# Slot order in a fused image and text transformer block: row maxima, projections, sum of values, drain

## The chip, the cores and the metric

The kernel runs on one core of a Trainium2 chip. The metric is the device time of one execution in microseconds (us). The core has five engines that work side by side and wait for each other by semaphores: TensorE (PE, matrix products and transposes; PEld is its weight load), VectorE (DVE), ScalarE (ACT), GpSimd (POOL) and SyncE (SP), which here only issues transfers.

## The reference

16 images with 16 text rows each go through four stages. All is float32.

```
h = edges(gray(x)) + text rows                      # per image 256 rows of pixels and 128 of text, 256 wide
h = h + attention(layernorm(h))                     # 16 heads of 16, window of 128 keys, 1e-9 added to each weight
n = layernorm(h); h = h + (n, and gelu(n @ W) where score(n) is in the top 75%)
n = layernorm(h); h = h + C @ scan(B @ n) + D * n   # state space, solved with turned cumulative sums
n = layernorm(h); h = h + shared_ffn(n) + sum over top 2 of 8 experts of gate * ffn_e(n)
```

The 1e-9 that is added to each attention weight is computed as one product: a matrix of 1e-9 times the values, summed over the keys ("sum of values").

## The kernel before, in words

Work on the images is laid over each other. Round b of a loop does the attention of image b, the "chain" of image b-1 (router score and block, state space, logits and the first layer of the shared network), the "late" part of image b-2 (second layer of the shared network in six steps called down, ranks of its rows in the experts' lists, and dispatch, which writes those ranks to memory with six indirect transfers on POOL), and the "head" of image b+1 (gray, edges by a convolution, layernorm, projections). Rounds 2 to 14 are a loop; rounds 0, 1, 15, 16 and 17 are written out, and the parts that have no image are left out of them. Round 1 has chain and head, but no late part; round 15 has no head; round 16 has only chain and late part. After them the experts run over chunks of 256 rows.

A round has 33 slots (0 to 32). Each engine has a function `sequence` which goes through the slots and calls what belongs to each; nothing reorders them, so an engine that waits holds up all that stands behind. The semaphores say what each call waits for.

What one attention slot does: slot s makes the scores of unit s (two heads of one tile of 128 rows) on PE, their row maxima on DVE (`mx`), the exponential on ACT (`prob`); slot s also turns the weights of unit s-2 on PE (L1548), which ACT copies out (`pT`), and every second slot multiplies them with the values (L1561, "value products"). Scores of unit s need the exponential of unit s-2, because there are two PSUM buffers. In slots 14 and 22 PE turns the finished context (`cx`, L1576), in slots 16, 24 and 31 it multiplies it with the output matrix (`wo`, L1582).

Other calls that the change touches, by slot and line of the kernel before:

- slot 1: `turn_chain(b, 0)` (L1602) turns the normalised rows into PSUM banks 6 and 7 after the last hidden layer (`hid_ready`) of the image before has been read; slot 2: the router score (L1656), block products (L1607) and the sum of values (L1524), then the first step of down (L1629).
- slot 14: the input product of the state space (L1666, into banks 6 and 7) on PE; then on DVE four products that read it (L1200 to L1203) and signal `u_read`. Slots 15 to 18: the four quarters of the convolution (L1465) of image b+1 in the same banks; the first waits for `u_read`.
- slot 11 on DVE: `make_gray` (L1045 to L1051). Slots 19 to 21: the output product of the state space (L1677, L1678), then on DVE its addition (L1222), statistics (L1027, L1031), and `xn` (L1036), the normalised rows of image b+1, which PE turns in slot 22 (L1487).
- slot 26: the projection of the queries (L1493 with `wq`).
- round 16 and after: dispatch of image 14 stands first in POOL's round, ahead of the reciprocal root for the second layernorm (L604 to L614, `lnc`); ranks of image 15 come after all up products (L1616), and the list of rows per expert (L1374) after its last sum (L1261).

Of the kernel before, what the change touches and what calls it, by code (L numbers as in the profile page):

```python
# [16 lines left out]
NB = 16  # L17
IMG = 256
D = 256
KB = D // P  # L20
NT = 3
# [34 lines left out]
UPS = {30: (0,), 31: (1,)}  # L56
UPS_LAST = (2, 3, 4, 5, 6, 7)
# [19 lines left out]
def build(nc, t):  # L77
    with ExitStack() as ctx:
# [490 lines left out]
        def _(pool):  # L569
# [93 lines left out]
            def sequence(b, att, late, chain, head):  # L663
                if late:
                    dispatch(b - 2)
                if chain:
                    chain_deviations(b - 1, 1)
                    direct_term(b - 1)
                    states(b - 1)
                if head:  # L670
                    head_deviations(b + 1)
                if chain:
                    chain_deviations(b - 1, 2)
                    shared_residual(b - 1)
# [60 lines left out]
        def _(act):  # L735
# [107 lines left out]
            def sequence(b, att, late, chain, head, first_weights=False):  # L843
                for s in range(SLOTS):
# [21 lines left out]
                    if chain and s == TURN2:  # L866
                        turned_rows(b - 1, 2)
                    for f in UPS.get(s, ()) if chain else ():
# [17 lines left out]
            gate_ratio(NB - 1)  # L886
# [38 lines left out]
        def _(dve):  # L925
# [234 lines left out]
            def chain(b, s):  # L1160
# [58 lines left out]
                if s == OUT + 1:  # L1219
# [5 lines left out]
                    dve.wait_ge(h3_ready.sem, h3_ready.at(b, 1))  # L1225
                    chain_rows(b, 2)
# [73 lines left out]
            def sequence(b, att, late, chained, head, first=False, first_weights=False):  # L1300
                att_step.steps = 0
                for s in range(SLOTS):
# [8 lines left out]
                    if chained:  # L1311
# [3 lines left out]
                    if att:  # L1315
                        unit(b, s)
                    if late and s == RANKS + 1:
# [52 lines left out]
            shared_sum(NB - 1)  # L1370
            dve.wait_ge(route_loaded.sem, route_loaded.at(0, 16))
            for e in range(NE):
# [5 lines left out]
                elif e < NE - 1:  # L1378
                    link(ins, route_step, 0)
            ins.then_inc(slots_ready.sem, 1)  # L1380
# [59 lines left out]
        def _(pe):  # L1440
# [78 lines left out]
            def values_sum(b):  # L1519
# [3 lines left out]
                for i in range(NT):  # L1523
                    ins = pe.matmul(ps[:, 5, D:2 * D].rearrange("p (h d) -> p h d", h=NH), ones9[:], vaug[:, i, :, 0:DK],  # L1524
                                    start=(i == 0), stop=(i == NT - 1))
                ins.then_inc(sumv_done.sem, 1)

            def unit(b, s):
# [13 lines left out]
                if TURN <= s < NU + TURN:  # L1542
# [7 lines left out]
                    ins.then_inc(turned.sem, 1)  # L1550
                if PV <= s < NU + PV and (s - PV) % 2 == 1:
# [26 lines left out]
                if s in WO:  # L1578
                    i = WO.index(s)
                    pe.wait_ge(cxT_ready.sem, cxT_ready.at(b, i + 1))  # L1580
                    for k in range(KB):
                        ins = pe.matmul(ps[:, 5, D:2 * D], cxT[:, k], wo[:, k], start=(k == 0), stop=(k == KB - 1))  # L1582
                    ins.then_inc(wo_done.sem, 1)
# [4 lines left out]
            def turn_chain(b, n, head):  # L1588

                pe.wait_ge(xc_ready.sem, xc_ready.at(b, n + 1))  # L1590
                pe.wait_ge(xcT_ready.sem, xcT_ready.at(b, n))
                if n == 0:
                    pe.wait_ge(hid_ready.sem, hid_ready.at(b, 0))
# [6 lines left out]
                for k in range(KB):  # L1600
                    for i in range(NT):
# [47 lines left out]
            def chain(b, s, head):  # L1649
# [12 lines left out]
                if s == TURN1 + 2:  # L1662
# [26 lines left out]
            def sequence(b, att, late, chained, head, first=False):  # L1689
                for s in range(SLOTS):  # L1690
                    if first and s == 1:
# [3 lines left out]
                    if head and s == UP + 2:  # L1695
                        values(b + 1)
                    if att and s == BLOCK:
                        values_sum(b)
# [4 lines left out]
                    if chained and s == TURN0:  # L1703
                        turn_chain(b - 1, 0, head)
                    if att:
                        unit(b, s)
                    if late and s == RANKS:
# [13 lines left out]
                    if head and s == TURN2 - 1:  # L1721
                        queries(b + 1)
# [24 lines left out]
            sequence(1, True, False, True, True)  # L1747
# [3 lines left out]
            sequence(NB, False, True, True, False)  # L1751
            slot_ranks(NB - 1, False)
# [42 lines left out]

            turn_chunk(0)
# [79 lines left out]
```

## Time and profile before

| What | us |
|---|---|
| Median of 3 runs | 2193.5 |
| Lowest and highest | 2188.15 and 2195.46 |
| Profiled execution, its own time | 2192.07 |
| Its span (first to last instruction) | 2190.3 |
| PE busy in the span | 1965.9 (90%) |
| DVE busy | 1350.6 (62%) |
| ACT busy | 1079.5 (49%) |
| POOL busy | 819.2 (37%) |

Mean granted clock of TensorE was 0.969. (The mean is over the span.) A timeline row says when a group of instructions starts, how long it lasts together, and in square brackets how long the engine sat idle before it and which instruction ended that; a row without brackets had no such idle time. A row of the table by stretches gives for one stretch the busy time of each engine, the granted clock of TensorE as a share of full speed (1.00 is 2.4 GHz, 0.50 is 1.2 GHz), the busy share of the transfer engines and GB/s. "(x533)" counts instructions.

### The profile page before, as it was taken

How to read it: one execution, taken by the hardware profiler on the slowest of the kernel's cores; microseconds unless marked ns; L12 is line 12 of the kernel's file. 1: busy time of each engine (PE TensorE's matmuls, PEld its weight loads, DVE VectorE, ACT ScalarE, POOL GpSimd, SP SyncE). 2: the span in 40 equal slices, each digit the busy share in tenths (PEclk: the TensorE clock that was granted, in tenths of full speed). 3: DMA queues.
4: the chain of work that ended last, by engine and by line, in shares of the span. 5: the costliest groups of instructions: out<-in, count | busy, mean ns of one | idle time of the engine just before them, and what ended most of it. 6: DMA issues, size and time to landing. Idle time of an engine off the chain costs nothing.

```text
span 2190.3 us, 44925 instructions
## 1 busy us (share of the span) xinstructions
PE 1965.9 (90%) x13651; PEld 1559.6 (71%) x13652; DVE 1350.6 (62%) x3572; ACT 1079.5 (49%) x2513; POOL 819.2 (37%) x1535
## 2 busy tenths in 40 slices
PE   2879999999999999999999999985789999999997
PEld 1546666666666666666666666653689999999997
DVE  5647668577576685775766757643455565555654
ACT  0336455455554554555545555541355455555553
POOL 3113324334243233342432333322344545454454
PEclk8789999999999999999999999996899999999998
DMA  4220211211202112112021121110333232323322
GB/s 138 65 58 9 66 45 29 65 35 45 65 15 65 44 28 65 33 47 65 15 65 43 30 65 31 35 59 8 111 84 84 44 83 47 81 48 81 48 47 40
DMA packets 81090, 116.53 MB, mean 53 GB/s; under 512 B 20965, under 2 KB 61509, under 8 KB 78725
## 3 DMA queue, kind: packets, MB, share of 16 engines
q1 hardware_dynamic: 54948, 85.34, 14.1%
q0 software_dynamic: 23360, 27.91, 7.8%
q10 hardware_dynamic: 2736, 2.76, 0.4%
q8 instruction: 19, 0.31, 0.1%
q14 instruction: 27, 0.21, 0.0%
HBM read 51.58 MB, written 26.71 MB: 36 GB/s over the span
## 4 chain that ended last, share of the span: by engine, by line
PE 51%; DVE 16%; issue 14%; POOL 8%; DMA 5%; ACT 4%; POOLq 0%; DVEq 0%; SPq 0%; ACTq 0%
PE ps L1780 10%; PE ps L1616 8%; POOL slot_rows L658 4%; PE ps L1493 4%; PE ps L1792 3%; PE ps L1791 3%; PE ps L1793 3%; DVE mx L1119 2%; PE ps L1582 2%; PE ps L1465 2%; DMA result<-yb,idx_o 2%; PE ps L1607 2%; PE ps L1561 2%; PE ps L1548 2%; DMA slot_rows<-pay,row_i 2%
## 5 line engine op out<-in xcount | busy, mean ns | idle before, releaser
L793 ACT ACTIVATE prob<-ps,mx 128x256 f32<-128x256 f32 (+1 forms) x768 | 295.0, 443 | 254.9 <-DVE mx L1119 240.1
L897 ACT ACTIVATE hid_hi<-ps,b 128x256 fp32r<-128x256 f32 x408 | 205.8, 504 | 286.1 <-PE ps L1780 286.1
L1119 DVE TENSOR_REDUCE mx<-ps 128x2 f32<-128x512 f32 (+1 forms) x384 | 224.5, 594 | 116.0 <-PE ps L1540 107.3
L785 ACT ACTIVATE pT<-ps 128x512 f32<-128x512 f32 (+1 forms) x384 | 205.2, 534 | 123.9 <-PE ps L1548 120.5
L1395 DVE TENSOR_TENSOR hid_lo<-hid_full,hid_hi 128x256 fp32r<-128x256 f32 x408 | 172.3, 426 | 150.7 <-ACT hid_full L900 150.1
L1539 PE MATMUL ps<-ks,qs 96*128 96x512 f32 (+1 forms) x384 | 186.7, 487 | 63.9 <-ACT prob L793 51.0
L1791 PE MATMUL ps<-w_hi,hid_hi 128*128 128x256 f32 x816 | 232.3, 285 | 0.0
L1792 PE MATMUL ps<-w_lo,hid_hi 128*128 128x256 f32 x816 | 227.9, 279 | 0.0
L1793 PE MATMUL ps<-w_hi,hid_lo 128*128 128x256 f32 x816 | 227.9, 279 | 0.0
L900 ACT ACTIVATE hid_full<-ps,b 128x256 f32<-128x256 f32 x408 | 206.2, 505 | 0.0
L1548 PE MATMUL ps<-ident,prob 128*128 128x128 f32 x1280 | 204.8, 277 | 0.0
L658 POOL DMA_INDIRECT slot_rows<-pay,row_i x96 | 111.8, 1165 | 242.0 <-DVE tok L1289 217.6
L712 POOL DMA_INDIRECT result<-yb,idx_o x102 | 168.4, 1651 | 80.6 <-DVE yb L1412 37.8
L1629 PE MATMUL ps<-sw,hid 128*128 128x256 f32 x768 | 184.4, 385 | 1.6 <-ACT g L820 1.0
L1548 PEld LDWEIGHTS ps<-ident,prob 128*128 128x128 f32 x1280 | 164.9, 144 | 21.8 <-issue 1.6
L1616 PE MATMUL ps<-xcT,sw 128*128 128x384 f32 x512 | 172.2, 490 | 0.7 <-ACT hid L829 0.7
L1780 PE MATMUL ps<-xg_hi,w_hi 128*128 128x256 f32 x816 | 166.3, 285 | 3.0 <-DVE xg_lo L1388 1.7
L1780 PE MATMUL ps<-xg_lo,w_hi 128*128 128x256 f32 x816 | 165.5, 284 | 0.0
L1780 PE MATMUL ps<-xg_hi,w_lo 128*128 128x256 f32 x816 | 165.3, 284 | 0.0
L1629 PEld LDWEIGHTS ps<-sw,hid 128*128 128x128 f32 x768 | 140.0, 190 | 28.1 <-issue 11.2
L1791 PEld LDWEIGHTS ps<-w_hi,hid_hi 128*128 128x128 f32 x816 | 155.5, 191 | 0.0
L1792 PEld LDWEIGHTS ps<-w_lo,hid_hi 128*128 128x128 f32 x816 | 153.9, 189 | 0.0
(269 smaller groups left out, 4175.6 us busy)
## 6 DMA issues: line engine op xcount, KB each, us to landing
w_raw<-in_w SPq DMA_DIRECT2D x16, 1024.0 KB, 6.0
xin<-in_x SPq DMA_DIRECT2D x32, 384.0 KB, 3.6
qs<-q_hi SPq DMA_DIRECT2D x128, 96.0 KB, 2.1
ks<-k_hi SPq DMA_DIRECT2D x256, 48.0 KB, 2.1
qs<-q_lo SPq DMA_DIRECT2D x64, 96.0 KB, 2.1
ks<-k_lo SPq DMA_DIRECT2D x128, 48.0 KB, 2.1
xn_rows<-xc SPq DMA_DIRECT2D x16, 384.0 KB, 2.5
result<-h SPq DMA_DIRECT2D x16, 384.0 KB, 2.5
```

The source lines that it names most:

```text
L785: act.activation(pT[:, u % TB, :, k0:2, :], ps[:, 2 + u % 2, :].rearrange("p (h k q) -> p h k q", h=2, k=2)[:, :, k0:2, :], ACT.Copy).then ...
L793: ins = act.activation(prob[:, s % PB, hh, w], ps[:, s % 2, hh * 2 * P + w.start:(hh + 1) * 2 * P], ACT.Exp, bias=mx[:, s % 2, hh:hh + 1])
L897: act.activation(hid_hi[:, f], ps[:, f % 4, 0:CHUNK], ACT.Gelu_apprx_tanh, bias=b1[half][:, f:f + 1])
L900: act.activation(hid_full[:, f % 4], ps[:, f % 4, 0:CHUNK], ACT.Gelu_apprx_tanh, bias=b1[half][:, f:f + 1]).then_inc(ehid_ready.sem, 1)
L1119: dve.tensor_reduce(mx[:, s % 2], sc, AX_X, ALU.max, negate=True).then_inc(max_done.sem, 1)
L1548: ins = pe.transpose(ps[:, 2 + u % 2, (2 * hh + k) * P:(2 * hh + k + 1) * P], prob[:, u % PB, hh, k * P:(k + 1) * P], ident[:])
L1616: ins = pe.matmul(ps[:, 6 + f % 2, 0:T], sw1[:, k, f * P:(f + 1) * P], xcT[:, k], start=(k == 0), stop=(k == KB - 1))
L1629: ins = pe.matmul(tile_out(i), hid[:, f, i * P:(i + 1) * P], sw2[:, f], start=(f == 0), stop=(f == FB - 1))
L1780: ins = pe.matmul(ps[:, f % 4, 0:CHUNK], w[half][:, k, cols], x[:, k], start=(n == 0), stop=(n == len(terms) - 1))
L1791: pe.matmul(out, hid_hi[:, f, rows], w2_hi[half][:, f], start=(f == 0), stop=False)
L1792: pe.matmul(out, hid_hi[:, f, rows], w2_lo[half][:, f], start=False, stop=False)
L1793: ins = pe.matmul(out, hid_lo[:, f, rows], w2_hi[half][:, f], start=False, stop=(f == FB - 1))
```

## The change

On PE: (1) the output product `wo` of a slot stands ahead of its value products; (2) the projection of the queries stands ahead of slot 26's attention unit; (3) the input product of the state space is now a function of its own, `drive`, and stands behind slot 14's attention unit; (4) the first turn of the chain waits for the seventh hidden layer before it writes bank 6 and for the eighth only before bank 7; (5) the sum of values is made in two parts, one third in slot 1 and two thirds in slot 2; (6) in round 16 the ranks of image 15 stand behind the first up product, and the first turn of the experts waits for the last sum `h4_ready`.

On DVE: (7) in slots 14, 20 and 21 the row maximum stands ahead of the chain's work, and the third statistics (`chain_rows(b, 2)`) move from slot 20 to 21; (8) the last sum stands between the fourth and the fifth copy of the list.

On ACT: (9) the ratio of image 15's gates stands in slot 30 of round 16. On POOL: (10) in round 16 the dispatch stands behind the work on the states.

```diff
+LATER = (STATE, OUT + 1, OUT + 2)
@@ POOL, sequence
-                if late:
+                if late and att:
                     dispatch(b - 2)
                 if chain:
                     chain_deviations(b - 1, 1)
                     direct_term(b - 1)
                     states(b - 1)
+                if late and not att:
+                    dispatch(b - 2)
@@ ACT, sequence
+                    if first_weights and s == min(UPS):
+                        gate_ratio(b - 1)
...
-            gate_ratio(NB - 1)
@@ DVE, chain
                     dve.wait_ge(h3_ready.sem, h3_ready.at(b, 1))
+                if s == OUT + 2:
                     chain_rows(b, 2)
@@ DVE, sequence
-                    if chained:
+                    if chained and s not in LATER:
                         chain(b - 1, s)
                     if att and s == 2:
                         values_sum(b)
                     if att:
                         unit(b, s)
+                    if chained and s in LATER:
+                        chain(b - 1, s)
@@ DVE, the list
-            shared_sum(NB - 1)
...
+                if e == 3:
+                    shared_sum(NB - 1)
@@ PE, turn_chain
+                if n == 0 and not first:
+                    pe.wait_ge(hid_ready.sem, hid_ready.at(b - 1, FB - 1))
                 pe.wait_ge(xc_ready.sem, xc_ready.at(b, n + 1))
                 pe.wait_ge(xcT_ready.sem, xcT_ready.at(b, n))
-                if n == 0:
-                    pe.wait_ge(hid_ready.sem, hid_ready.at(b, 0))
...
                 for k in range(KB):
+                    if n == 0 and k == 1:
+                        pe.wait_ge(hid_ready.sem, hid_ready.at(b, 0))
@@ PE, sequence
+                    if head and s == TURN2 - 1:
+                        queries(b + 1)
                     if att and s == BLOCK:
-                        values_sum(b)
+                        values_sum(b, 1, NT)
...
                     if att:
                         unit(b, s)
+                    if att and s == TURN0:
+                        values_sum(b, 0, 1)
...
+                    if chained and s == TURN1 + 2:
+                        drive(b - 1)
...
-                    if head and s == TURN2 - 1:
-                        queries(b + 1)
...
+                    if last and s == min(UPS):
+                        slot_ranks(b - 1, False)
...
-            slot_ranks(NB - 1, False)
@@ PE, experts
+            pe.wait_ge(h4_ready.sem, h4_ready.at(NB, 0))
             turn_chunk(0)
```

PE in the loop, slots 13 to 15, before (`xcT,fb` is the input product of the state space, `ks,qs` and `mask_bf` the scores, `ident,prob` the turned weights, `pT,vaug` the value products, `gray_hi,band_hi` the first product of the convolution):

```order
L1548 MATMUL ps<-ident,prob 128x128 x4
L1666 MATMUL ps<-xcT,fb 128x384 x4
L1537 REGISTER_ALU
L1539 MATMUL ps<-ks,qs 128x512
L1540 MATMUL ps<-mask_bf,ident_bf 128x512
L1548 MATMUL ps<-ident,prob 128x128 x4
L1561 MATMUL ps<-pT,vaug 32x128 x8
L1576 MATMUL ps<-ident,cx 128x128 x2
L1537 REGISTER_ALU
L1539 MATMUL ps<-ks,qs 128x512
```

The same place of the changed kernel, and on to the convolution:

```order
L1557 MATMUL ps<-ident,prob 128x128 x4
L1576 MATMUL ps<-pT,vaug 32x128 x8
L1591 MATMUL ps<-ident,cx 128x128 x2
L1678 MATMUL ps<-xcT,fb 128x384 x4
L1546 REGISTER_ALU
L1548 MATMUL ps<-ks,qs 128x512
L1549 MATMUL ps<-mask_bf,ident_bf 128x512
L1557 MATMUL ps<-ident,prob 128x128 x4
L1468 REGISTER_ALU
L1473 MATMUL ps<-gray_hi,band_hi 128x512
```

The input product has gone behind slot 14's scores, turned weights, value products and `cx`; between it and the convolution only slot 15's scores and turned weights are left.

DVE in the loop, slots 20 and 21, before (`lnc` is the statistics of the chain, `xn` the rows of image b+1):

```order
L1222 TENSOR_TENSOR hc<-hc,ps 128x768
L1027 BN_STATS lnc<-hc 128x6 x3
...
L1031 BN_AGGR lnc<-lnc 128x2 x3
L1118 REGISTER_ALU
L1119 TENSOR_REDUCE mx<-ps 128x2
L1118 REGISTER_ALU
L1119 TENSOR_REDUCE mx<-ps 128x2
...
L1125 RECIPROCAL rden<-ps 128x16
L1127 TENSOR_TENSOR cx<-ps,rden 128x256
L1132 TENSOR_TENSOR cx<-cx,sumv 128x256
L1036 TENSOR_SCALAR xn<-h,ln 128x256 x3
```

And in the changed kernel:

```order
L1123 TENSOR_REDUCE mx<-ps 128x2
L1226 TENSOR_TENSOR hc<-hc,ps 128x768
L1122 REGISTER_ALU
L1123 TENSOR_REDUCE mx<-ps 128x2
L1128 REGISTER_ALU
L1129 RECIPROCAL rden<-ps 128x16
L1131 TENSOR_TENSOR cx<-ps,rden 128x256
L1136 TENSOR_TENSOR cx<-cx,sumv 128x256
L1031 BN_STATS lnc<-hc 128x6 x3
...
L1035 BN_AGGR lnc<-lnc 128x2 x3
L1040 TENSOR_SCALAR xn<-h,ln 128x256 x3
```

Slot 20's maximum has gone ahead of the addition, and the statistics stand between `cx` and `xn`.

## Rows read from the trace of the kernel before

**Rows 1.** Busy times of one round: from:to, us, then each engine, clock, DMA.
```profile
678.46:766.27 87.81, 82.12 (x533) 58.16 (x534) 59.98 (x164) 45.87 (x102) 31.14 (x75) 1.00 0.18 45
```
**Rows 2.** Timeline of PE, slots 14 to 16 of a loop round.
```profile
707.93 2.75 PE L1666 MATMUL ps<-xcT,fb 128*128 128x384 f32 x8
711.77 0.50 PE L1539 MATMUL ps<-ks,qs 96*128 96x512 f32 x1 [1.09 <-ACT prob L793]
...
713.64 0.48 PE L1539 MATMUL ps<-ks,qs 96*128 96x512 f32 x1
...
714.54 0.48 PE L1465 MATMUL ps<-gray_hi,band_hi 128*128 128x512 f32 x1
...
716.21 0.49 PE L1539 MATMUL ps<-ks,qs 96*128 96x512 f32 x1 [0.24 <-ACT prob L793]
```
**Rows 3.** Timeline of DVE, the same stretch.
```profile
710.16 1.28 DVE L1119 TENSOR_REDUCE mx<-ps 128x2 f32<-128x512 f32 x2
...
713.92 0.55 DVE L1203 TENSOR_TENSOR rot<-ps,turn 128x384 f32<-128x384 f32 x1
```
**Rows 4.** Timeline of DVE, slots 20 and 21.
```profile
729.46 0.95 DVE L1222 TENSOR_TENSOR hc<-hc,ps 128x768 f32<-128x768 f32 x1 [0.34 <-PE ps L1678]
...
731.80 1.25 DVE L1119 TENSOR_REDUCE mx<-ps 128x2 f32<-128x512 f32 x2
```
**Rows 5.** Timeline of PE, slots 21 to 26.
```profile
731.17 0.48 PE L1539 MATMUL ps<-ks,qs 96*128 96x512 f32 x1
...
733.38 0.49 PE L1539 MATMUL ps<-ks,qs 96*128 96x512 f32 x1 [1.06 <-ACT prob L793]
...
735.32 0.82 PE L1487 MATMUL ps<-ident,xn 128*128 128x128 f32 x6
...
738.09 0.65 PE L1561 MATMUL ps<-pT,vaug 128*32 128x128 f32 x16 [0.61 <-ACT pT L785]
...
741.00 0.64 PE L1561 MATMUL ps<-pT,vaug 128*32 128x128 f32 x16 [0.76 <-ACT pT L785]
```
**Rows 6.** Timeline of PE, slots 1 and 2 of the next round.
```profile
764.41 0.88 PE L1602 MATMUL ps<-ident,xc 128*128 128x128 f32 x6 [0.43 <-ACT hid L829]
...
770.25 1.46 PE L1524 MATMUL ps<-vaug,ones 128*128 128x256 f32 x6
```
**Rows 7.** Timeline of PE in round 15, scores of slot 19 and the turned weights behind.
```profile
1424.56 0.56 PE L1539 MATMUL ps<-ks,qs 96*128 96x512 f32 x1 [2.18 <-ACT prob L793]
...
1425.36 1.06 PE L1548 MATMUL ps<-ident,prob 128*128 128x128 f32 x4
```
**Rows 8.** Busy times and clock of the stretch that begins there.
```profile
1424.40:1428.20 3.80, 3.65 (x11) 2.91 (x12) 0.85 (x2) 3.14 (x8) 0.00 (x0) 0.56 0.02 4
```
**Rows 9.** Timeline of POOL in round 16: dispatch, second and third reciprocal root.
```profile
1467.25 1.12 POOL L658 DMA_INDIRECT slot_rows<-pay,row_i  x1 [13.83 <-DVE tok L1289]
...
1476.14 0.20 POOL L604 TENSOR_SCALAR lnc<-lnc 128x3 f32<-128x3 f32 x1 [1.43 <-DMA slot_rows<-pay,row_i]
...
1496.96 1.19 POOL L632 TENSOR_TENSOR st<-rot 128x384 f32<-128x384 f32 x1
...
1506.35 0.20 POOL L604 TENSOR_SCALAR lnc<-lnc 128x3 f32<-128x3 f32 x1 [8.20 <-DVE lnc L1031]
```
**Rows 10.** Timeline of DVE from the second statistics of round 16 to the first chunk.
```profile
1472.33 0.21 DVE L1031 BATCH_NORM_AGGREGATE lnc<-lnc 128x2 f32<-128x6 f32 x2
...
1530.63 0.20 DVE L1269 TENSOR_TENSOR picked<-hot,ps 128x48 f32<-128x48 bf16 x1 [10.73 <-PE ps L1645]
...
1542.06 0.95 DVE L1261 TENSOR_TENSOR h<-hb,ps 128x768 f32<-128x768 f32 x1 [6.21 <-PE ps L1629]
1547.08 0.21 DVE L1374 COPY flat<-table 128x96 int32<-128x96 int32 x1 [4.07 <-DMA table<-slot_rows]
...
1554.45 0.21 DVE L1374 COPY flat<-table 128x96 int32 x1 [0.77 <-DVE flat L1374]
...
1557.17 0.69 DVE L1386 CAST xg_hi<-ps 128x512 fp32r<-128x512 f32 x1 [2.50 <-PE ps L1764]
```

More of the change, by code:

```diff
@@ L1517, in values, with values_sum @@
                 ins.then_inc(proj_done.sem, 1)
-            def values_sum(b):
+            def values_sum(b, first, last):
                 pe.wait_ge(v_ready.sem, v_ready.at(b, 1))
                 pe.wait_ge(h1_ready.sem, h1_ready.at(b, 0))
-                for i in range(NT):
+                for i in range(first, last):
                     ins = pe.matmul(ps[:, 5, D:2 * D].rearrange("p (h d) -> p h d", h=NH), ones9[:], vaug[:, i, :, 0:DK],
                                     start=(i == 0), stop=(i == NT - 1))
-                ins.then_inc(sumv_done.sem, 1)
+                if last == NT:
+                    ins.then_inc(sumv_done.sem, 1)
             def unit(b, s):
@@ L1550, in unit @@
                     ins.then_inc(turned.sem, 1)
+                if s in WO:
+                    i = WO.index(s)
+                    pe.wait_ge(cxT_ready.sem, cxT_ready.at(b, i + 1))
+                    for k in range(KB):
+                        ins = pe.matmul(ps[:, 5, D:2 * D], cxT[:, k], wo[:, k], start=(k == 0), stop=(k == KB - 1))
+                    ins.then_inc(wo_done.sem, 1)
                 if PV <= s < NU + PV and (s - PV) % 2 == 1:
@@ L1577, in unit, with turn_chain @@
                     ins.then_inc(cx_turned.sem, 1)
[L1578 to L1583, printed above, removed]
             def tile_out(i):
                 return ps[:, 6 + i // 2, (i % 2) * D:(i % 2 + 1) * D]
-            def turn_chain(b, n, head):
+            def turn_chain(b, n, head, first=False):
+                if n == 0 and not first:
+                    pe.wait_ge(hid_ready.sem, hid_ready.at(b - 1, FB - 1))
                 pe.wait_ge(xc_ready.sem, xc_ready.at(b, n + 1))
                 pe.wait_ge(xcT_ready.sem, xcT_ready.at(b, n))
-                if n == 0:
-                    pe.wait_ge(hid_ready.sem, hid_ready.at(b, 0))
                 if n == 1:
@@ L1661, in chain, with drive @@
                     block_tile(2).then_inc(block_done.sem, 1)
-                if s == TURN1 + 2:
+            def drive(b):
                     pe.wait_ge(xcT_ready.sem, xcT_ready.at(b, 2))
@@ L1687, in logits, with sequence @@
                     ins.then_inc(logit_done.sem, 1)
-            def sequence(b, att, late, chained, head, first=False):
+            def sequence(b, att, late, chained, head, first=False, last=False):
                 for s in range(SLOTS):
-                    if first and s == 1:
+                    if first and not chained and s == 1:
                         pe.wait_ge(mats_read.sem, mats_read.at(0, 1))
@@ L1703, in sequence @@
                     if chained and s == TURN0:
-                        turn_chain(b - 1, 0, head)
+                        turn_chain(b - 1, 0, head, first)
                     if att:
                         unit(b, s)
+                    if att and s == TURN0:
+                        values_sum(b, 0, 1)
                     if late and s == RANKS:
@@ L1746, in _ @@
             pe.wait_ge(late_loaded.sem, late_loaded.at(0, NLATE))
-            sequence(1, True, False, True, True)
+            sequence(1, True, False, True, True, first=True)
             with pe.Fori(2, NB - 1) as b:
@@ L1750, in _ @@
             sequence(NB - 1, True, True, True, False)
-            sequence(NB, False, True, True, False)
-            slot_ranks(NB - 1, False)
+            sequence(NB, False, True, True, False, last=True)
             for n in range(2 * NT):
```

## The prediction

> **What bounds the kernel now.** I read the timeline of PE for the router score first: it comes back every 87.81 us, which is the length of one loop round. The table by stretches for one round [rows 1] shows PE busy for 82.12 of 87.81 us at a granted clock of 1.00, DVE 59.98, ACT 45.87, POOL 31.14. So in the loop PE is the bound, and all that any reordering can win is its idle time, 87.81 - 82.12 = 5.7 us a round. Then PE's timeline, bracket by bracket, shows where that lies: 1.09 us ahead of slot 14's scores and 0.24 ahead of slot 16's [rows 2], 1.06 ahead of slot 22's and 0.61 and 0.76 ahead of two value products [rows 5], 0.43 ahead of the chain's first turn [rows 6]. The rest is in places that the change leaves alone. The reader is to see in these rows who ended each wait: ACT's exponential, which itself waits for DVE's maximum. Last, the drain of round 16, where PE mostly waits and POOL and DVE set the end [rows 9, 10].
>
> **The change part by part, in the loop.** Fourteen rounds (1 to 14) have both chain and head. The rows are of one of them; the others start the same calls with the same waits.
>
> *Input product behind slot 14's unit.* Before, it runs from 707.93 for 2.75 us, and then PE still waits 1.09 us, until 711.77, for the exponential of slot 12 [rows 2]. That one is late because DVE reaches the maxima of slots 12 and 13 only at 710.16, behind make_gray [rows 3]. The input product was the filler of this wait. Without it PE has nothing from about 707.9 to 711.77: 3.84 us idle where there were 1.09. Scores, turned weights, value products and `cx` of slot 14 then take the same 1.87 us as now (711.77 to 713.64 [rows 2]), the input product runs 713.64 to 716.39. Now what is queued behind: DVE's four products that read it. Each starts 0.465 us after the one before and the last lasts 0.55 [rows 3], 1.95 together, so they end at about 718.4 instead of 714.47. The convolution's first product waits for them: it started at 714.54, now it starts at 718.4 [rows 2], 3.86 later; what PE can put in between (scores and turned weights of slot 15, 713.64 to 714.54, 0.9 us) is over at 717.3. Slot 16's 0.24 us wait goes. The price is 3.86 - 0.24 = +3.6 us a round. Slot 14's maximum ahead of the four products gains nothing here: its exponential is early, but PE isn't waiting for it any longer. Bounds: at best the moved product fills as much as before, 0; at worst 3.9.
>
> *Maxima of slots 20 and 21 ahead, statistics behind `cx`.* The 1.06 us wait for the exponential of slot 20 goes [rows 5]. But take T, the end of the state's output product (DVE's addition starts at 729.46 [rows 4]). Before, addition and statistics took 731.80 - 729.46 = 2.34 us [rows 4], and from 731.80 to the turn of `xn` at 735.32 [rows 5] it was 3.52, together T + 5.86. Now slot 21's maximum stands behind the addition and waits for its scores, which start at 731.17 [rows 5] and are read at about 731.9, T + 2.4; the maximum takes 0.6; then `cx` and `xn`, 3.52 less the two maxima, 2.3; and between them the statistics, 2.34 less the addition of 0.95, 1.4. That is T + 6.7. What ends last is DVE's `xn`, and PE meets a wait of about 2 us at that turn. Price +0.9 us. Bounds -1.06 (if `xn` is in time) and +1.5.
>
> *`wo` and queries ahead of value products.* Both put ready work into waits for ACT's copy: 0.61 and 0.76 us [rows 5]. Both have their inputs in time (the output product's context was turned two slots before, the rows of image b+1 two slots before too). -1.4 us; bounds -1.4 and 0. The copy of the context behind the value products comes up to 2.75 us later, but is used only behind the key projection of equal length.
>
> *First turn in two halves, sum of values in two parts.* Half of the turn goes into the 0.43 us wait, one third of the sum of values (1.46 us [rows 6]) into the wait for ACT's copy behind it. The block output, its gelu on ACT and the exponential that slot 2 waits for then come some 0.3 us earlier, and the first step of down waits for the same gelu. -0.4 us; bounds -0.8 and 0.
>
> Sum of a round: 3.6 + 0.9 - 1.4 - 0.4 = +2.7 us. Fourteen rounds: +38. Round 0 has only the pair of projections, round 15 has no gray and no convolution, so that its input product costs about what its other waits give back; I take 0 for both.
>
> *The clock.* In round 15 PE stood idle 2.18 us, and right behind it four turned weights took 1.06 us instead of 0.60 [rows 7]; the stretch has a granted clock of 0.56 [rows 8], which is the lower level, 1.2 GHz, in nearly all of it. In 3.8 us with PE busy for 3.65, about half of the work was lost, 1.7 us. The changed loop has 3.8 us of idle in slot 14 and some 2 us in slot 22, in every round, ahead of work on which the round's length hangs; the round before has none over 1.09 and stays at 1.00 [rows 1]. I take one such fall a round: 14 x 1.7 = +24 us. Bounds 0 and two falls, +48.
>
> The Trainium skill, in "TensorE: Matmul & The Clock Gate", section "HAM oscillation — how this bites in real kernels", says that a wait which comes back in each turn of a loop sets TensorE's clock back in each turn, rather than once. By it the 24 us stand; by the loop of this trace alone, which shows no fall at its own shorter waits, they would be 0. It speaks against this change, and the trace has one place, round 15, that bears it out.
>
> **The drain.** The second statistics of round 16 were ready at 1472.54 [rows 10], yet the reciprocal root began at 1476.14, because the dispatch stood ahead [rows 9]: -3.6 us. The dispatch now follows the states, which end at 1498.15 - 3.6 = 1494.5. It took from 0.8 before 1467.25 to 1476.0, 9.5 us [rows 9], so it holds POOL until 1504.0, and the third root starts there instead of at 1506.35: of 3.6 us, 2.35 are left. That is the wait which takes the removed one's place. The ranks of image 15 waited 10.73 us for PE's up products [rows 10] and now don't; the list's table is there some 13 us earlier, at about 1533. What is late next is the last sum, now between the fourth and fifth copy: it waits for the last down step, 1542.06 - 2.9 = 1539.2 (2.35 plus about 0.5 for the table load of the gates that is gone). Then 0.95 for the sum and four copies at (1554.45 - 1547.08) / 7 = 1.05 us: 1544.3, where the first chunk's rounding starts instead of at 1557.17 [rows 10]. That is -12.9 us. The gather, 8.9 us from the first copy to its turned rows, ends before that. I take -13; bounds -5 (if the gather or the chunk's weights end last) and -16. The experts behind are untouched.
>
> **Sum.** The profiled execution took 2192.07 us, 1.4 under the median of 2193.5, so I add to the median: 38 + 24 - 13 = +49, 2242 us.
>
> **Rivals.**
> A, the forecast: 2242.
> B, the clock does not fall: 38 - 13 = +25, 2218. For it: 1252 us of loop at full clock in spite of 5.7 us idle a round. Against: [rows 7, 8].
> C, it falls twice a round, in slots 14 and 22: +24 more, 2266. For it: the second wait, of about 2 us, is nearly as long as the 2.18 us in [rows 7].
> D, faster: the input product behind the unit costs nothing, because slot 14's scores are released early enough. It decides itself at 707.9 + 2.75 = 710.7: if the exponential of slot 12 came before that, the product would have delayed the scores and its new place would win. Then the loop has only the fills, 14 x (1.4 + 0.4) = -25, and the drain -13: 2155. For it: round 15, which has no make_gray. Against: in the loop DVE starts the maximum of slot 12 at 710.16 [rows 3], so the exponential can't be earlier than 711.7.
> E, loop and drain cancel: input product and `xn` cost under 2 us a round more than the fills give, clock at 1.00: within 7 us of before.
>
> **How the numbers follow.** Chances: A 0.45, B 0.21, C 0.13, D 0.15, E 0.06. A change under 0.3% (6.6 us) can't be told from none here. Slower by more: A, B, C, 0.79. Within: 0.06. Faster: 0.15. The range 2200 to 2268 holds A, B and C and leaves out D and E.
>
> **What would show it.** PE's timeline in the loop should have a wait of over 3 us ahead of slot 14's scores, one of about 1.2 us ahead of the convolution, and one of 1.5 to 2.5 us, ended by `xn`, ahead of its turn; no waits ahead of the value products of slots 24 and 26. The router score should come back every 90.5 us with the clock at 1.00, and 92 or more with stretches at 0.50. In the drain the third root should start when the dispatch ends, and the first chunk's rounding right behind the last copy. I am wrong if slot 14's scores wait no longer than before, if the round is under 88 us, or if the drain gives under 5 or over 20.

## The result, and the profile after

| | before | changed |
|---|---|---|
| Median, us | 2192.47 (4 runs) | 2241.76 (4 runs) |
| Lowest and highest | 2188.15 and 2195.46 | 2237.35 and 2242.2 |
| Ratio with its 95% interval | | 1.0222 [1.02, 1.0244] |
| Profiled execution, its own time | 2192.07 | 2242.2 |
| Its span | 2190.3 | 2240.4 |
| Mean granted clock | 0.969 | 0.955 |

The kernel is 49.3 us slower; 2242 was forecast. (In the experiments below, one execution of e4_filler, the profiled one, took 2501.43 us at a granted clock of 0.773 where its four others took 2235.8 to 2239.53; it is left out of the ratio.)

To see whether the loss came about for the forecast's reasons, the span of the profiled execution is cut at PE's router scores, which begin each round's chain, and at DVE's first rounding of the experts' rows:

| Stretch of the span, us | before | changed | difference | forecast |
|---|---|---|---|---|
| to the router score of round 1 | 153.45 | 152.70 | -0.8 | |
| rounds 1 to 14 | 1227.6 | 1288.5 | +60.9 | +62 |
| round 15 | 77.48 | 82.85 | +5.4 | 0 |
| round 16 and the list | 98.67 | 86.58 | -12.1 | -13 |
| experts | 633.13 | 629.77 | -3.4 | 0 |

Rounds 1 to 14 lost 60.9 / 14 = 4.35 us each. From the router score of round 2 to that of round 15 a round takes 92.21 us instead of 87.84.

PE from slot 13's turned weights to the convolution in slot 15, one loop round of the changed kernel, its timeline; it answers to [rows 2]:

```profile
732.99 0.60 PE L1557 MATMUL ps<-ident,prob 128*128 128x128 f32 x4
737.27 0.51 PE L1548 MATMUL ps<-ks,qs 96*128 96x512 f32 x1 [3.68 <-ACT prob L796]
...
739.83 3.77 PE L1678 MATMUL ps<-xcT,fb 128*128 128x384 f32 x8
743.14 0.69 PE L1548 MATMUL ps<-ks,qs 96*128 96x512 f32 x1
743.90 0.60 PE L1557 MATMUL ps<-ident,prob 128*128 128x128 f32 x4
745.64 0.50 PE L1473 MATMUL ps<-gray_hi,band_hi 128*128 128x512 f32 x1 [1.14 <-DVE rot L1207]
```

The wait of 1.09 us has become 3.68 us, since the 2.75 us of input product that stood in it are gone. The product now takes 3.77 us instead of 2.75, and behind it the convolution has its 1.14 us wait for DVE's four products. DVE at the same place, answering to [rows 3]:

```profile
735.05 0.69 DVE L1055 TENSOR_TENSOR gray_lo<-xin,gray_hi 128x512 fp32r<-128x512 f32 x1
735.66 1.28 DVE L1123 TENSOR_REDUCE mx<-ps 128x2 f32<-128x512 f32 x2
...
743.63 0.56 DVE L1204 TENSOR_TENSOR rot<-ps,turn 128x384 f32<-128x384 f32 x1 [4.90 <-PE ps L1678]
```

The maxima of slots 12 and 13 still stand behind make_gray: the wait of 3.68 us ends when the chain gray_lo, maximum, exponential is through. The price of the moved product shows in DVE's 4.90 us of idle time behind them. The table by stretches (busy time of each engine, then granted clock) says why the product took 3.77 us:

```profile
703.97:795.86 91.89, 83.59 (x529) 58.62 (x534) 61.12 (x164) 45.73 (x102) 30.98 (x75) 0.98 0.17 43
...
735.90:739.30 3.40, 2.03 (x22) 1.29 (x22) 2.68 (x6) 2.87 (x7) 0.00 (x0) 0.88 0.01 3
739.30:742.70 3.40, 3.40 (x12) 2.14 (x9) 0.00 (x0) 0.89 (x3) 0.00 (x0) 0.62 0.01 3
```

The clock fell from 2.4 to 1.2 GHz, here behind the wait and for most of the second stretch. It did so once in each of the 13 rounds of the loop: eight times for 3.4 us and five times for 6.8, and then it stood at 1.2 GHz from 1.7 to 1.9 us before the end of the wait. That is 61.4 us in all; the loop before has no such stretch.

PE in slots 21 and 22, answering to [rows 5]:

```profile
766.63 0.88 PE L1495 MATMUL ps<-ident,xn 128*128 128x128 f32 x6 [1.85 <-DVE xn L1040]
...
769.65 0.64 PE L1576 MATMUL ps<-pT,vaug 128*32 128x128 f32 x16
...
773.46 0.65 PE L1576 MATMUL ps<-pT,vaug 128*32 128x128 f32 x16
```

The turn of `xn` waits 1.85 us, where the scores of slot 22 waited 1.06; the two value products have lost their waits of 0.61 and 0.76. The two orders of DVE behind the first row, with the statistics (L1031) ahead of `xn`:

```profile
760.46 0.69 DVE L1123 TENSOR_REDUCE mx<-ps 128x2 f32<-128x512 f32 x1 [0.74 <-PE ps L1549]
761.07 0.94 DVE L1226 TENSOR_TENSOR hc<-hc,ps 128x768 f32<-128x768 f32 x1
762.52 0.69 DVE L1123 TENSOR_REDUCE mx<-ps 128x2 f32<-128x512 f32 x1 [0.51 <-remote]
...
764.21 1.07 DVE L1031 BATCH_NORM_STATS2 lnc<-hc 128x6 f32<-128x256 f32 x3
...
765.55 1.03 DVE L1040 TENSOR_SCALAR xn<-h,ln 128x256 f32<-128x256 f32 x3
```

DVE goes idle ahead of both maxima (`remote`: the profile names no releaser): in order, it waits for scores, ahead of slot 20's maximum while the addition could run and ahead of slot 21's while the statistics could. `xn` itself could not run yet: POOL ends its root at 763.83. But then the statistics stand between `cx` and `xn`.

The drain, POOL and then DVE, answering to [rows 9] and [rows 10]:

```profile
1558.51 1.19 POOL L633 TENSOR_TENSOR st<-rot 128x384 f32<-128x384 f32 x1
1559.86 2.87 POOL L659 DMA_INDIRECT slot_rows<-pay,row_i  x1 [0.16 <-issue]
...
1570.47 0.20 POOL L605 TENSOR_SCALAR lnc<-lnc 128x3 f32<-128x3 f32 x1 [1.43 <-DMA slot_rows<-pay,row_i]
```

```profile
1584.73 0.20 DVE L1274 TENSOR_TENSOR picked<-hot,ps 128x48 f32<-128x48 bf16 x1 [0.72 <-PE ps L1656]
...
1606.16 0.95 DVE L1266 TENSOR_TENSOR h<-hb,ps 128x768 f32<-128x768 f32 x1 [3.50 <-PE ps L1640]
1607.03 0.20 DVE L1380 COPY flat<-table 128x96 int32 x1
...
1610.38 0.21 DVE L1380 COPY flat<-table 128x96 int32 x1 [0.77 <-DVE flat L1380]
1610.63 0.69 DVE L1394 CAST xg_hi<-ps 128x512 fp32r<-128x512 f32 x1
```

The third root starts when the dispatch ends, the ranks wait 0.72 us instead of 10.73, the last sum is what comes late (it waits 3.50 us), and the first rounding stands right behind the last copy.

### The profile page after: what moved, and what is told of

Read it like the earlier page. It is cut to its first block, busy times and chain, and to the rows that moved or that the text cites. A ratio compares the mean times of both kernels' runs of the same rounds, so it can differ in the third digit from the quotient of the medians.

```text
span 2240.4 us, 44872 instructions
## 1 busy us (share of the span) xinstructions
PE 1986.6 (89%) x13572; PEld 1564.3 (70%) x13652; DVE 1366.8 (61%) x3572; ACT 1071.2 (48%) x2509; POOL 816.4 (36%) x1535
## 4 chain that ended last, share of the span: by engine, by line
PE 51%; DVE 17%; issue 13%; POOL 9%; DMA 4%; ACT 2%; POOLq 1%; DVEq 1%; another core or an unknown queue 0%; SPq 0%; ACTq 0%
PE ps L1797 9%; POOL slot_rows L659 4%; PE ps L1501 4%; PE ps L1808 3%; PE ps L1809 3%; PE ps L1810 3%; PE ps L1473 3%; PE ps L1557 3%; PE ps L1678 2%; PE ps L1576 2%; PE ps L1548 2%; PE ps L1627 2%; PE ps L1618 2%; DMA result<-yb,idx_o 2%; PE ps L1640 2%
## 5 line engine op out<-in xcount | busy, mean ns | idle before, releaser
L1557 PE MATMUL ps<-ident,prob 128*128 128x128 f32 x1280 | 209.3, 281 | 7.6 <-ACT prob L796 1.4
L1548 PEld LDWEIGHTS ps<-ks,qs 96*128 96x128 f32 x384 | 75.1, 196 | 118.4 <-ACT prob L796 82.5
```

What stands on the lines that cost most here:

```text
L1548: pe.matmul(dst, qs[:, r, m, i * P:(i + 1) * P], ks[:, r, :, m, keys], start=True, stop=False)
L1557: ins = pe.transpose(ps[:, 2 + u % 2, (2 * hh + k) * P:(2 * hh + k + 1) * P], prob[:, u % PB, hh, k * P:(k + 1) * P], ident[:])
```

## The experiments

Theory 1 is the forecast: the input product behind slot 14's unit, `xn` behind the statistics and one fall of the clock a round cost, the fills and the drain give. Rivals were that one of them costs or gives nothing. "Round" is the mean of rounds 2 to 14 between router scores; "at 1.2 GHz" is the time at the lower clock in those 13 rounds; every ratio is to the kernel before, run on the same chip as the experiment (three chips, on which its median was 2191.74 to 2194.03 us).

| Kernel | median, us | ratio [95%] | round | at 1.2 GHz |
|---|---|---|---|---|
| before | 2192.47 | | 87.84 | 0 |
| changed | 2241.76 | 1.0222 [1.02, 1.0244] | 92.21 | 61.4 |
| e1_input_back | 2189.2 | 0.9981 [0.9968, 0.9993] | 88.34 | 37.5 |
| e2_input_only | 2276.96 | 1.0383 [1.0359, 1.0407] | 94.05 | 68.3 |
| e3_drain_only | 2180.1 | 0.9945 [0.9928, 0.9963] | 87.89 | 0 |
| e4_filler | 2238.28 | 1.0199 [1.0176, 1.0223] | | |
| e5_statistics_back | 2237.84 | 1.021 [1.0193, 1.0227] | 92.19 | 88.8 |
| e6_statistics_back_filler | 2199.32 | 1.0043 [1.0027, 1.006] | 89.50 | 0 |
| e7_fills_and_drain | 2151.21 | 0.9821 [0.9805, 0.9838] | 86.03 | 0 |
| e8_gray_early | 2148.23 | 0.9811 [0.9795, 0.9828] | 85.00 | 0 |
| e9_two_fillers | 2215.82 | 1.0105 [1.0089, 1.0121] | 90.38 | 0 |
| e10_gray_early_first_round | 2138.55 | 0.9758 [0.9744, 0.9771] | 85.00 | 0 |
| e11_gray_early_product_behind | 2169.04 | 0.9897 [0.9882, 0.9913] | 87.17 | 0 |

### e1_input_back: the input product in its old place

```diff
 PE, sequence
                         chain(b - 1, s, head)
+                    if chained and s == TURN1 + 2:
+                        drive(b - 1)
...
-                    if chained and s == TURN1 + 2:
-                        drive(b - 1)
```

> The changed kernel with one thing undone: the input product of the state space stands ahead of slot 14's unit again. Theory 1 (the moved product costs some 3.6 us a round in waits and 1.7 in a clock fall): the wait of 3.7 us ahead of slot 14's scores and the 1.1 us one ahead of the convolution go, 14 x 5.3 = 74 us, so about 2168 us. Theory 2 (the order of maxima, addition and statistics on DVE costs the time, and the product's place is neutral): within 7 us of the changed kernel, 2235 to 2249.

Measured 2189.2 us: 53 us less than the changed kernel, but 21 over the 2168 of theory 1. PE in slot 22, its timeline, and the stretch behind that wait:

```profile
740.34 1.38 PE L1495 MATMUL ps<-ident,xn 128*128 128x128 f32 x6 [1.84 <-DVE xn L1040]
741.37 0.78 PE L1548 MATMUL ps<-ks,qs 96*128 96x512 f32 x1
...
742.39 1.81 PE L1557 MATMUL ps<-ident,prob 128*128 128x128 f32 x8
```

```profile
740.30:743.70 3.40, 3.36 (x15) 2.86 (x16) 1.28 (x2) 1.95 (x5) 2.46 (x14) 0.54 0.00 0
```

The six turns take 1.38 us where the changed kernel's took 0.88: the fall of the clock has not gone, it has moved to the wait for `xn`, 11 times in 13 rounds. The product's place is the largest part of the loss; that it alone makes the clock fall is refuted.

The same trace prices one fall. The two of its 13 rounds that had none took 86.99 and 86.85 us; the eleven others, with 3.4 us at 1.2 GHz each, took 88.48 to 89.24, most of them 88.5. One fall of 3.4 us so costs 1.6 us.

### e2_input_only: the kernel before, with the product behind slot 14's unit

```diff
 PE, the chain
-                if s == TURN1 + 2:
+            def drive(b):
...
 PE, sequence
                         edge(b + 1, s - CONV, chained)
+                    if chained and s == TURN1 + 2:
+                        drive(b - 1)
```

> The kernel before with the input product alone moved behind slot 14's unit. Theory 1: 2192 + 14 x 5.3 = 2267 us, a round of about 93 us, clock below 1.00 in the loop. Theory 2: within 7 us of the kernel before.

Measured 2276.96 us, 10 over theory 1's 2267, with 6.2 us a round more than before. One part of the change is worse than the whole. The clock stands at 1.2 GHz for 5.25 us a round (68.3 / 13). The 0.24 us wait ahead of slot 16's scores is still there (0.23), as it is in e11; in the changed kernel, e6 and e9, where slot 14's maximum stands ahead of the four products, it is gone.

### e3_drain_only: only items 6, 8, 9 and 10 of the change

```diff
 POOL, sequence
-                if late:
+                if late and att:
                     dispatch(b - 2)
...
+                if late and not att:
+                    dispatch(b - 2)
 PE, sequence
+                    if last and s == min(UPS):
+                        slot_ranks(b - 1, False)
```

(with the moved last sum, the gates' ratio and the experts' wait for it as in the change)

> The kernel before with the parts of round 16 and after alone (dispatch behind the states, gate ratio and ranks early, last sum between the copies, first turn of the experts waits for it). Theory 1: -13 us, 2179, loop rounds unchanged at 87.8. The rival (the table is not what the first chunk waits for): under 5 us gained.

Measured 2180.1 us. Its span is 12.9 us under before, its rounds are the same (87.89). The drain's gain stands alone and does not need the loop's parts.

### e4_filler: the input product issued twice in slot 14

```diff
 PE, sequence
                         chain(b - 1, s, head)
+                    if chained and head and s == TURN1 + 2:
+                        drive(b - 1, False)
```

(`drive(b - 1, False)` issues the same products without the signal; the real ones follow behind the unit.)

> The changed kernel with the input product issued twice in the rounds that have a head: once as a filler ahead of slot 14's unit, whose result nobody reads, and once behind it as in the changed kernel. PE then works in the 3.7 us stretch, but what waits for what is the same. If the clock fall is a cost of its own (theory 1), 1.7 us a round or 24 us come back: about 2218 us, and the granted clock in slots 14 and 15 is 1.00. If the waits alone cost the time, 2242 us.

Measured 2238.28 us, 20 over theory 1's value. No row of its trace is read. With e1 in view, the wait of 1.85 us for `xn` was still there and could still bring the clock down; e6 and e9 test that.

### e5_statistics_back and e6_statistics_back_filler: DVE's old order in slots 20 and 21

```diff
-LATER = (STATE, OUT + 1, OUT + 2)
+LATER = (STATE,)
...
                     dve.wait_ge(h3_ready.sem, h3_ready.at(b, 1))
-                if s == OUT + 2:
                     chain_rows(b, 2)
```

e6 has this and e4's filler too.

> The changed kernel with slots 20 and 21 on DVE as before (addition and statistics ahead of the maxima); slot 14 stays changed. Theory 1: the 1.85 us wait for xn goes, the 1.06 us one for the exponential of slot 20 comes back, 0.9 us a round less, and the clock still falls in slot 14: 2242 - 14 x 0.9 - 3 = 2226 us. Theory 2 (the order of slots 20 and 21 carries most of the loss): under 2205 us.

> The same, with the input product issued once more ahead of slot 14's unit in rounds with a head, its result overwritten by the real one. What waits for what stays as in the kernel without the filler, and no wait over 1.3 us is left in the loop. If a clock fall costs time of its own: clock 1.00 in the loop and 14 x 2.4 = 34 us less than without the filler (4.9 us at half rate a round), some 2192 us. If the waits alone cost the time: the same as without the filler, 2226 us.

e5 measured 2237.84 us, 12 over its expected value; e6 2199.32, 7 over. PE at slot 14, e5 and then e6:

```profile
739.05 0.79 PE L1547 MATMUL ps<-ks,qs 96*128 96x512 f32 x1 [3.67 <-ACT prob L796]
```

```profile
720.75 0.50 PE L1547 MATMUL ps<-ks,qs 96*128 96x512 f32 x1 [1.09 <-ACT prob L796]
...
727.49 0.50 PE L1472 MATMUL ps<-gray_hi,band_hi 128*128 128x512 f32 x1 [1.15 <-DVE rot L1207]
```

In e5 the scores behind the wait take 0.79 us, at 1.2 GHz, in e6 0.50. In both the exponential is equally late, and DVE's order is the same: the filler changes nothing but that PE is busy. So 92.19 - 89.50 = 2.69 us a round is the clock's price alone, for 88.8 / 13 = 6.8 us at the lower clock. And e5's loop is no shorter than the changed kernel's, though an `xn` wait is gone from it: its falls last longer (6.8 instead of 4.7 us a round) and cost 2.69 instead of 1.83. Why they last longer isn't settled.

### e7_fills_and_drain: the product and all three slots of DVE as before, the rest as changed

```diff
-LATER = (STATE, OUT + 1, OUT + 2)
+LATER = ()
```

(with e1's edit and e5's second one)

> The changed kernel with the input product ahead and all three DVE slots as before; wo and queries ahead of the value products, the first turn in two halves, the sum of values in two parts and the drain stay. Theory 1: 14 x (1.4 + 0.4) = 25 us from the fills and 14 from the drain, 2154 us, clock 1.00 in the loop. Rival (the fills are given back at the next wait): 2180 us, the drain's gain alone.

Measured 2151.21 us, faster than both kernels. `wo` and the queries ahead of value products, the half turn and the split sum of values give 87.84 - 86.03 = 1.81 us a round.

### e8_gray_early and e10_gray_early_first_round: room for the maximum of slot 12

```diff
+GRAYS = (4, 5, 6, 7, 8)
...
-                    if head and s == GRAY_AT:
-                        make_gray(b + 1)
+                    if head and first and s == GRAY_AT:
+                        make_gray(b + 1)
+                    if head and not first and s in GRAYS:
+                        make_gray(b + 1, GRAYS.index(s))
```

e7, with make_gray's five operations spread over slots 4 to 8 instead of in one block in slot 11. e8 does so in round 0 too, e10 as in the diff.

> The kernel of fills and drain, with make_gray's five operations in slots 4 to 8, one in each, instead of all in slot 11. If make_gray is what holds the exponential of slot 12 back (theory 1), the 1.09 and 0.24 us waits of slots 14 and 16 go: 14 x 1.3 = 19 us less, 2135 us. Rival: the maxima of slots 4 to 8 come later and PE waits there instead, no gain or a loss.

> e8_gray_early, but in round 0, where the image of round 1 is not loaded by slot 4, make_gray stays in slot 11 as one block. Theory 1: the 10 us that e8 lost in round 0 come back and the loop keeps its 85.00 us: 2138. Rival: the image of round 1 is late anyway and something else of round 0 takes the wait: no gain, 2148.

e8 measured 2148.23 us, 13 over its expected value. Its round is 85.00, 1.03 us under e7's where 1.3 were expected: the waits ahead of slots 14 and 16 are gone, but PE now waits 0.56 us for DVE ahead of a step of down. And its first router score comes 10.6 us later than e7's (162.99 against 152.39), most of it because DVE waits 6.97 us in slot 4 of round 0 for an image still on its way. e10 gives these back: 2138.55 us, the fastest kernel of this study, 54 us under the one before.

### e9_two_fillers: the changed kernel with both long waits filled

```diff
 PE, sequence
+                    if chained and head and s == TURN1 + 2:
+                        drive(b - 1, False)
...
+                    if chained and head and s == ROWS + 3:
+                        drive(b - 1, False, True)
```

(The second call issues half of the input product, ahead of the turn of `xn`.)

> The changed kernel, with two groups of products on PE whose results nobody reads: the input product a second time in slot 14 ahead of the scores, and half of it once more in slot 22 ahead of the turn of xn. Both orders of DVE and PE stay as in the changed kernel, so its waits stay in length, but PE is not idle in the two longest. Theory 1 (a fall of the clock costs the changed kernel 1.7 to 2 us a round beyond its waits): the router score comes back every 90.0 to 90.7 us at a granted clock of 1.00 instead of every 92.21, time 2212 to 2220. Theory 2 (the half clock lies beside waits and costs nothing): 92.2 a round and 2242, although the clock stands at 1.00. Rival on e4_filler: if one of the two waits was not filled long enough, the clock still falls and the time stays above 2235.

Measured 2215.82 us, round 90.38, clock 1.00 in the whole loop. Its PE and its stretch of one round:

```profile
722.29 0.50 PE L1548 MATMUL ps<-ks,qs 96*128 96x512 f32 x1 [1.09 <-ACT prob L796]
...
729.03 0.50 PE L1473 MATMUL ps<-gray_hi,band_hi 128*128 128x512 f32 x1 [1.14 <-DVE rot L1207]
...
750.02 0.87 PE L1495 MATMUL ps<-ident,xn 128*128 128x128 f32 x6 [0.55 <-DVE xn L1040]
```

```profile
688.98:779.27 90.29, 86.19 (x545) 59.74 (x545) 61.12 (x164) 45.72 (x102) 31.06 (x75) 1.00 0.17 44
```

PE is busy for 2.6 us more than in the changed kernel's round above (86.19 against 83.59), and the round is on average 1.83 us shorter. Work that nobody reads makes the kernel 26 us faster: 14 x 1.83 is the price of the falls in the changed kernel's full rounds. (In round 15, which has no filler, e9 stands at 1.2 GHz for 20.5 us, and takes 85.28 us.) e9 has only the second filler more than e4 and is 22 us faster, so e4's miss was most likely a fall that the first filler had left: the mean clock of e4's four other executions is 0.960 to 0.962, between the changed kernel's 0.955 to 0.957 and e9's 0.968 to 0.972.

### e11_gray_early_product_behind: e10 with the product behind slot 14's unit

> e10_gray_early_first_round with the input product of the state space behind slot 14's unit, as in the change. It tests whether the place of the product is right by itself once DVE is free for slot 12's maximum. Theory 1 (two waits make its price: the filler of slot 14's wait, which is gone here, and the convolution, which waits for DVE's four products that read it): slot 14's scores wait under 0.6 us, but the convolution's first product still waits 1 to 1.9 us, so 1.0 to 1.9 us a round more than e10, 2152 to 2165. Rival (make_gray alone made the price, rival D of the prediction): same as e10 or faster, 2130 to 2140. Theory 3 (the whole price stays): 3.5 us a round more, 2187.

(The edit is e2's, made to e10.) Measured 2169.04 us, 2.17 us a round more than e10 (87.17 - 85.00), above theory 1's 1.9. PE at slots 14 to 16, first e10, then e11:

```profile
692.55 2.75 PE L1688 MATMUL ps<-xcT,fb 128*128 128x384 f32 x8
694.84 0.69 PE L1558 MATMUL ps<-ks,qs 96*128 96x512 f32 x1
...
697.44 0.60 PE L1567 MATMUL ps<-ident,prob 128*128 128x128 f32 x4
697.80 0.48 PE L1483 MATMUL ps<-gray_hi,band_hi 128*128 128x512 f32 x1
```

```profile
705.03 0.50 PE L1558 MATMUL ps<-ks,qs 96*128 96x512 f32 x1
...
706.99 2.75 PE L1688 MATMUL ps<-xcT,fb 128*128 128x384 f32 x8
709.27 0.69 PE L1558 MATMUL ps<-ks,qs 96*128 96x512 f32 x1
...
711.77 0.50 PE L1483 MATMUL ps<-gray_hi,band_hi 128*128 128x512 f32 x1 [1.15 <-DVE rot L1216]
...
713.46 0.50 PE L1558 MATMUL ps<-ks,qs 96*128 96x512 f32 x1 [0.25 <-ACT prob L797]
```

Slot 14's scores (694.84 in e10, 705.03 in e11) wait for nothing in either; the convolution still waits. The brackets add up to 1.40 us of the 2.17. The rest lies where one instruction used to start before the end of the one ahead: in e10 the convolution starts 0.24 us before the turned weights end at 698.04, and slot 14's scores 0.46 us before the product does; in e11 no such overlap is left at these places.

e11 leaves slot 14's maximum where it was, so its 2.17 us hold the 0.25 us wait of slot 16, which e6's 3.47 (below) do not. With that taken off, some 1.9 us of the product's price remain when make_gray is out of the way, and some 1.5 hang on make_gray; this is an estimate that takes the terms to add up. Rival D is refuted at its own best condition.

## Why the prediction was right, point by point

The loop's terms a round, each the difference of two kernels. The four add up to the whole difference by the way the pairs are chosen; what the experiments test is the size of each. e6 and e9 also have their fillers, which run in waits:

| Term | forecast | measured | between |
|---|---|---|---|
| `wo`, queries, first turn, sum of values | -1.8 | -1.81 | e7, before |
| input product behind, slot 14's maximum ahead | +3.6 | +3.47 | e6, e7 |
| maxima 20 and 21 ahead, statistics later | +0.9 | +0.88 | e9, e6 |
| the clock | +1.7 | +1.83 | changed, e9 |
| sum | +4.4 | +4.37 | changed, before |

- **The input product.** Right in size and mechanism: it was the filler of a wait that make_gray sets, and behind it stand DVE's products and the convolution. Slot 14's maximum ahead was not tested alone, but that it "gains nothing here" seems wrong: in both kernels that move the product without it, slot 16's wait stays, 0.23 us in e2 and 0.25 in e11. The forecast took that wait as gone and gave no reason.
- **The statistics.** Right where the clock stays at 2.4 GHz; e1's two rounds without a fall, 86.92 us on average, are e7's 86.03 and 0.88 more. Where the clock falls, the term is not additive: undone in the changed kernel (e5) it gives 0.02 us a round, since the falls become longer.
- **The clock.** The likeliest case, one fall a round, came out: after the 3.68 us wait, in all 13 rounds. Its price was taken from round 15 ([rows 7, 8]) as 1.7 us for 3.8 us of stretch; e1 has 1.6 for 3.4, so the price was right. The length was not foreseen. In the changed kernel the seven rounds behind the first with 3.4 us at 1.2 GHz take 91.9 us, 1.6 over e9's 90.3, and those with 6.8 take 92.4 to 92.7, some 2.3 over: part of the longer ones lies in the wait itself, where PE has no work that it could slow down. The mean is 1.83 us for 4.7; in e5, where all 13 last 6.8 us, it is 2.69. That the mean came to the forecast's 1.7 is in part luck. Rival B, no falls, is refuted. Rival C, a second fall behind the 1.85 us wait, did not come about in the changed kernel, but e1 shows that the wait can bring one.
  The Trainium skill's rule in "TensorE: Matmul & The Clock Gate", section "HAM oscillation — how this bites in real kernels", is that such a wait brings the clock down in every turn of a loop; the 13 falls in 13 rounds of the changed kernel agree with it, and behind e1's wait of 1.84 us there were 11.
- **Round 15.** Wrong: the step that failed is "I take 0 for both". Its reason, "its input product costs about what its other waits give back", held: e5, with the product in its new place, has 76.30 us there, under the 77.48 of before. But DVE's new order in slots 20 and 21 was not priced in this round, and the changed kernel lost 5.4 us there. The kernels with that order take 82.22 (e1), 82.85 and 85.28 us (e9) in round 15, those with the old one 76.30 (e5), 76.31 (e6) and 76.71 (e7). DVE in round 15, the changed kernel and then e5:

```profile
1496.91 0.21 DVE L1035 BATCH_NORM_AGGREGATE lnc<-lnc 128x2 f32<-128x6 f32 x2
...
1501.60 2.19 DVE L1040 TENSOR_SCALAR xc<-hc,lnc 128x256 f32<-128x256 f32 x3 [0.99 <-POOL lnc L615]
```

```profile
1493.73 0.21 DVE L1035 BATCH_NORM_AGGREGATE lnc<-lnc 128x2 f32<-128x6 f32 x2
...
1500.15 1.16 DVE L1040 TENSOR_SCALAR xc<-hc,lnc 128x256 f32<-128x256 f32 x3
```

  Round 15 begins at 1441.20 in the changed kernel and at 1442.87 in e5. Counted from there, the statistics are through 4.8 us later than in e5, so POOL's root too; `xc` starts 3.1 us later (60.40 for 57.28) and takes 2.19 us instead of 1.16. POOL's next operation starts with it here, and 1.75 us ahead of it in e5. (In the loop of the kernel before, each of the three parts of `xc` takes 0.41 us alone, and 0.70 to 0.82 beside an addition of the same size on POOL.) POOL in the changed kernel:

```profile
1501.45 2.19 POOL L649 TENSOR_TENSOR hb<-hc,sb_row 128x256 f32<-128x256 f32 x3
```

  PE waits 1.44 us for an exponential whose maximum stands behind the statistics, and 1.20 for `xc`, where e5 has neither wait (it has one of 1.07 us before, which the changed kernel lacks), and behind them its clock falls:

```profile
1498.62 0.66 PE L1557 MATMUL ps<-ident,prob 128*128 128x128 f32 x4 [1.44 <-ACT prob L796]
...
1503.84 0.87 PE L1613 MATMUL ps<-ident,xc 128*128 128x128 f32 x6 [1.20 <-DVE xc L1040]
...
1507.91 2.77 PE L1627 MATMUL ps<-xcT,sw 128*128 128x384 f32 x4
```

```profile
1502.20 0.87 PE L1612 MATMUL ps<-ident,xc 128*128 128x128 f32 x6
...
1505.58 1.46 PE L1626 MATMUL ps<-xcT,sw 128*128 128x384 f32 x4
```

  At the turn of `xc` PE is 3.3 us behind e5, and the last 3.2 us of the 6.5 between the two are lost behind it, where the clock stands at 1.2 GHz for 6.8 us and e5's for none. In the loop the same delay is hidden by the turn of `xn` and the queries' projection, which round 15 doesn't have: there the cover was gone, and the forecast didn't ask. In all the clock stood at 1.2 GHz for 13.7 us in this round, 3.4 before: the other 6.8 us lie at a wait of 2.43 us, which e5 has as well, with 3.4 us.
- **The drain.** -12.1 for -12.9. Its steps came in the forecast order. Round 16 begins 65.5 us later in the changed kernel, so the last sum, forecast for 1539.2, was due at 1604.7 and came at 1606.16; the first rounding came at 1610.63 for 1609.8. The third root starts at 1570.47 for 1569.5: POOL's first indirect transfer takes 2.87 us, where it took 1.12 in [rows 9]. From the root to the last sum it is 35.69 us, and it was 35.71 before (1506.35 to 1542.06), so the "about 0.5 for the table load of the gates that is gone" did not come. These two make the last sum 1.5 us late; 0.6 of it comes back up to the first rounding.
- **The experts.** -3.4 for 0. Nothing in them was changed but the first wait. With the same instructions they take 629.8 to 633.1 us in the twelve traces read, e3 632.0. The clock is not what differs: it stands at 1.2 GHz for 24.2 us of them before and for 24.3 in the changed kernel. The cause stays open.
- The errors outside the loop, +5.4, +0.9, -3.4 and -0.8, nearly cancel. That the total is within 1 us of the forecast is in part luck. That the loop is within 1.1 of its 62 us rests on waits that were each forecast and found, and, for the clock's share, on the mean length of a fall.

## What to carry to other kernels

In queues that run in order, an instruction that looks early may be what fills a wait: before moving it, read which wait stands behind it and who ends it, then follow its own readers to the next user of the same banks. A wait made longer can cost twice, once as idle time and once as clock, and the test for the second is cheap: issue work that nobody reads into the wait, and see whether the loop gets shorter. A move that is hidden in the full rounds must be priced again in the rounds that lack the covering work. The best version keeps the change's fills and drain, leaves the product and DVE's order alone, and takes away the cause of the late maximum: 2138.55 us.

## What the runs showed that was not expected

- The clock fell at waits of 1.84 us (e1, 11 of 13 rounds; the two others had the same wait); waits of 1.09 with 1.07 and 1.15 us in the same round (e6) left it at 1.00. Behind the changed kernel's 1.85 us wait it did not fall, in rounds where it had fallen before in slot 14. So the length of a wait alone does not decide it; what does was not tested.
- The length of a fall is 3.4 or 6.8 us in the loop, and changes with small edits elsewhere (4.7 us a round in the changed kernel, 5.25 in e2, 6.8 in e5).
- POOL's first indirect transfer of the same dispatch took 1.12 us behind a wait and 2.87 us right behind its work on the states. In the second place DVE runs a subtraction of 128x2048 (3.07 us, from 1558.77) beside it; which of the two made it longer was not tested.
